# The next batch's layer norm and transposes, moved to other places of an attention kernel's fixed order

## The chip, the cores and the metric

One Trainium2 chip, one core of it. The metric is the device time in microseconds (us) of one execution. The kernel before was timed three times: 2115.77, 2119.26 and 2119.72 us, median 2119.26.

## The reference

Eight batches (graphs) of 1024 tokens with 512 features; 16 heads of 32 features. A token attends to those tokens for which its row of `adj` is 1.

```python
h = relu(layernorm(x))                     # over the 512 features
q, k, v = h @ Wq + bq, h @ Wk + bk, h @ Wv + bv
scores = einsum(q, k) * 32 ** -0.5, -inf where adj == 0
out = softmax(scores) @ v                  # per head
return x + (out @ Wo + bo)
```

## The kernel before

`fast_attention` does the work (a second function, `general_attention`, runs only if a check at the end finds the inputs too large; here its instructions are skipped). Every engine has its own program, written by hand as the same sequence of steps, and the engines meet through semaphores (`wait_ge`, `then_inc`).

**Units and steps.** A batch is four units (`UNITS`, `up` = 0 to 3) of four heads each. A unit is 32 steps (`TILES`, `j` = 0 to 31): two sweeps of 16, one for each half of the queries; within a sweep a step is one tile of 128 keys (`kt`, 0 to 7) for one pair of heads. Batch 0 is written out, batches 1 to 6 are a loop (`Fori`), batch 7 is written out again, so the kernel returns to the start of the loop's body five times.

**The attention of a step.** TensorE (PE) multiplies the scores of step j+1 while it is in step j (`scores`, L679, two matmuls of 512 columns). VectorE (DVE) subtracts the mask and writes the tile to an eight-slot ring (`masked`, L903), ScalarE (ACT) takes the exponential in place (`exp`, L768), GpSimd (POOL) adds four of the eight key tiles up (`sums`, L1077). The products with v (`weighted`, L692, "p0" to "p7") and the row sums (`denominators`, L703, "dA", "dB", "d6", "d7") come as blocks at fixed steps of a sweep; `BLOCKS` puts them at r = 6, 10, 14, 16 and 18, so the last two lie in the next sweep or in the next unit:

```python
BLOCKS = {6: ("p0", "p1"), 10: ("p2", "p3", "dA"), 14: ("p4", "p5"), 16: ("p6", "dB", "d6"), 18: ("p7", "d7")}
```

They are float32 products; each that the code writes stands as two records in the profile.

**The chunks.** Everything else of PE is put in pieces between these steps, after the blocks of a step. Unit u computes, as chunks, what unit u+1 needs: q and k for its four heads (`PROJ`: 12 matmuls of 512 columns for each half of the tokens, so 48 in all, L652), v (96 matmuls of 128 columns, L659) and a bound on the norms (`NORMS`, L662). Units 0 and 1 also multiply the output projection of the batch before ("y", eight chunks of 12, L666). Unit 3 also transposes the next batch's normalised x ("t", eight chunks of four transposes, L648), since its own q, k and v are those of the next batch's unit 0. `chunk_list` gives the order of a unit's chunks, `chunk_plan` the step of every piece: t chunks by the table `T_AT`, the others spread evenly over the steps `SLOTS` (steps 1 to 28 with no block), in unit 3 over `AFTER_T` (those from 13 on). Two PSUM banks serve the chunks by turns, so a chunk waits until the one two before it has been read.

**After a chunk.** `high` on ACT (L774 for t, L780 for q and k, L784 for v) writes the fp16 upper part in the chunk's last step, `low` on DVE the remainder (L912 for t one step later, L916 for q and k two steps later), `square` on ACT (L792) one step after a q or k chunk. q and k then travel: three steps after the second half of q or of k, SyncE (SP) waits for `low` and stores the part to DRAM (`store_parts`, L505); five steps after, it waits for that store and loads it back in another layout by four transfers of 256 KB (`load_stack`, L510). The first scores of the next unit, issued in step 31, wait for all eight of these loads.

**The next batch's x.** `x_in` has four slots for eight tiles of tokens. SP loads tiles (`load_x`, L501), DVE computes statistics (`statistic`, L935) in unit 2, steps 1, 3, ..., 15, and the means in step 21, ACT the reciprocal deviations in step 23, DVE the shifts in step 25. ACT normalises in place (`normalise`, L817) in steps 27 to 30 of unit 2 (tiles 0 to 3) and 5 to 8 of unit 3 (tiles 4 to 7). Each statistic and each transpose is followed, one step later on SP, by a wait for it and the load of another tile into the slot. ACT also turns the next batch's adjacency into the mask (`to_mask`, L823): eight tiles in steps 17 to 30 of unit 3, eight in steps 1 to 13 of unit 0.

Of the kernel before, what the change touches and what calls it, by code (L numbers as in the profile page):

```python
# [4 lines left out]
B, S, D, H, P = 8, 1024, 512, 16, 128  # L5
# [286 lines left out]
NORMS_AT = 29  # L292
T_AT = [1, 3, 4, 5, 7, 8, 9, 11]
AFTER_T = [j for j in SLOTS if j >= 13]
STATS_AT = [2 * t + 1 for t in range(QT)]
MEANS_AT, RSTD_AT, SHIFT_AT = 21, 23, 25
NORMALISE_AT = {(2, 27): 0, (2, 28): 1, (2, 29): 2, (2, 30): 3, (3, 5): 4, (3, 6): 5, (3, 7): 6, (3, 8): 7}
# [4 lines left out]
def chunk_list(up, first, last):  # L302
    if up == UNITS - 1:
        return [] if last else [("t", t) for t in range(QT)] + PROJ + [NORMS]
# [23 lines left out]
def chunk_plan(up, first, last):  # L328

    chunks = [c for c in chunk_list(up, first, last) if c != NORMS]  # L330
    if not chunks:
        return {}
    plan = spread_out([c for c in chunks if c[0] != "t"], AFTER_T if up == UNITS - 1 else SLOTS)
    if up == UNITS - 1:
        plan.update({at: [("t", t, 0, PIECES["t"])] for t, at in enumerate(T_AT)})
    return {**plan, NORMS_AT: [(*NORMS, 0, PIECES["n"])]}

# [49 lines left out]
def fast_attention(nc, x, adjT, Wq, bq, Wk, bk, Wv, bv, Wo, bo, ident, headones, out, parts, flag):  # L387
    ctx = ExitStack()
    with ctx:
# [109 lines left out]
        def _(sp):  # L499
# [49 lines left out]
            def graph(b, first, last):  # L549
                for up in range(UNITS):  # L550
                    U = unit_no(b, up)
                    for j in range(TILES):
# [26 lines left out]
                        if up == 2:  # L579
                            for t, at_ in enumerate(STATS_AT):  # L580
                                if at_ == j - 1:
                                    sp.wait_ge(s["x_stats"], (b + 1) * QT + t + 1)
                                    load_x(b + 1, (t + X_SLOTS) % QT)
                        if up == UNITS - 1:
                            for t, at_ in enumerate(T_AT):
                                if at_ == j - 1:
                                    sp.wait_ge(s["chunk_ready"], chunk_no(ALL, b, up, first, ("t", t)) + 1)
                                    load_x(*((b + 1, t + X_SLOTS) if t + X_SLOTS < QT else (b, t + X_SLOTS - QT)))
# [174 lines left out]
        def _(act):  # L763
# [62 lines left out]
            def graph(b, first, last):  # L826
                for up in range(UNITS):
                    U = unit_no(b, up)
                    for j in range(TILES):
# [20 lines left out]
                        if up == 2 and j == RSTD_AT:  # L850
                            rstds(b + 1)
# [34 lines left out]
        def _(dve):  # L886
# [74 lines left out]
            def graph(b, first, last):  # L961
                for up in range(UNITS):
                    U = unit_no(b, up)
                    for j in range(TILES):
# [16 lines left out]
                        if up == 2 and not last:  # L981
                            if j in STATS_AT:
                                statistic(b, first, b + 1, STATS_AT.index(j))
                            if j == MEANS_AT:
# [155 lines left out]
```

## Time and profile before

| what | us |
|---|---|
| median of three executions | 2119.26 |
| the profiled execution | 2117.94 |
| its span, from the first to the last record | 2116.0 |
| PE busy | 1947.0 (92%) |
| DVE busy | 1545.7 (73%) |
| ACT busy | 1478.1 (70%) |
| POOL busy | 1295.6 (61%) |
| SP's transfers (of 16 engines' span) | 34.7% |
| mean granted clock of TensorE | 0.978 of full speed |

The profiled execution's own time is 1.9 us above its span and 1.3 us below the median. A matmul's end is modelled, so a busy PE is not a PE at its peak; here its matmuls follow one another at the spacing that the chain of waits shows for them, and the time that PE is not busy is where it waits. In the traces `L12` is line 12 of the kernel, `tile<-tiles` what an instruction writes and reads.

### The profile page before, as it was taken

How to read it: one execution, taken by the hardware profiler on the slowest of the kernel's cores; microseconds unless marked ns; L12 is line 12 of the kernel's file. 1: busy time of each engine (PE TensorE's matmuls, PEld its weight loads, DVE VectorE, ACT ScalarE, POOL GpSimd, SP SyncE). 2: the span in 40 equal slices, each digit the busy share in tenths (PEclk: the TensorE clock that was granted, in tenths of full speed). 3: DMA queues.
4: the chain of work that ended last, by engine and by line, in shares of the span. 5: the costliest groups of instructions: out<-in, count | busy, mean ns of one | idle time of the engine just before them, and what ended most of it. 6: DMA issues, size and time to landing. Idle time of an engine off the chain costs nothing.

```text
span 2116.0 us, 40441 instructions
## 1 busy us (share of the span) xinstructions
PE 1947.0 (92%) x14336; PEld 779.1 (37%) x14336; DVE 1545.7 (73%) x1587; ACT 1478.1 (70%) x1765; POOL 1295.6 (61%) x581
## 2 busy tenths in 40 slices
PE   3799999999899998999989999899989999999987
PEld 2333334333344333443334433343333333333422
DVE  5688857787667875778757787578866688677783
ACT  3577866778667786568866788667876678666772
POOL 0367748566567655657656576475656676475674
PEclk9999999999999999999999999999999999999998
DMA  5423234232443324333342334413444233441212
GB/s 175 120 80 94 87 105 135 61 110 76 116 120 89 101 76 126 95 91 95 101 125 75 91 105 116 126 55 91 114 117 111 74 96 97 110 130 46 61 31 80
DMA packets 103222, 206.61 MB, mean 98 GB/s; under 512 B 11616, under 2 KB 11744, under 8 KB 103008
## 3 DMA queue, kind: packets, MB, share of 16 engines
q1 hardware_dynamic: 103008, 203.80, 34.7%
q8 instruction: 129, 2.11, 0.4%
q14 instruction: 85, 0.70, 0.1%
HBM read 153.43 MB, written 50.33 MB: 96 GB/s over the span
## 4 chain that ended last, share of the span: by engine, by line
PE 75%; DVE 7%; DMA 6%; issue 6%; ACT 3%; POOL 1%; SPq 1%; DVEq 0%; ACTq 0%; POOLq 0%
PE ps L692 19%; PE ps L679 19%; PE ps L652 13%; PE ps L703 10%; PE ps L666 6%; PE ps L659 6%; DVE ring L903 4%; DMA k_stack<-k_parts 3%; DMA k_parts<-k_part 2%; ACT ring L768 1%; ACT hT_hi L774 1%; DVE oT_lo L958 1%; DVE k_part L916 1%; POOL acc L1077 1%; SPq L510 1%
## 5 line engine op out<-in xcount | busy, mean ns | idle before, releaser
L903 DVE TENSOR_TENSOR ring<-ps,mask 128x1024 f32<-128x1024 f32 x1024 | 1235.9, 1219 | 492.9 <-PE ps L679 479.7
L768 ACT ACTIVATE ring<-ring 128x1024 f32<-128x1024 f32 x1024 | 1068.3, 1051 | 445.8 <-DVE ring L903 435.5
L1077 POOL TENSOR_TENSOR acc<-ring 128x1024 f32<-128x1024 f32 x256 | 604.4, 2373 | 768.7 <-ACT ring L768 768.5
L679 PE MATMUL ps<-q_stack,k_stack 128*128 128x512 f16 x2048 | 614.5, 385 | 104.8 <-DVE ring L903 47.4
L1077 POOL TENSOR_TENSOR acc<-acc,ring 128x1024 f32<-128x1024 f32 x256 | 611.5, 2410 | 0.0
L692 PE MATMUL ps<-ring,v_sb 128*32 128x512 f32 x4096 | 517.3, 612 | 0.0
L679 PEld LDWEIGHTS ps<-q_stack,k_stack 128*128 128x128 f16 x2048 | 157.3, 98 | 505.4 <-DVE ring L903 240.4
L692 PEld LDWEIGHTS ps<-ring,v_sb 128*32 128x32 f32 x4096 | 101.5, 110 | 257.1 <-issue 229.6
L703 PE MATMUL ps<-acc,ones 128*32 128x512 f32 x1024 | 137.7, 606 | 0.0
L703 PE MATMUL ps<-ring,ones 128*32 128x512 f32 x1024 | 134.6, 595 | 0.0
L659 PE MATMUL ps<-wv_hi,hT_lo 128*128 128x128 f16 x1024 | 105.6, 219 | 0.0
L659 PE MATMUL ps<-wv_lo,hT_hi 128*128 128x128 f16 x1024 | 104.5, 219 | 0.0
L659 PE MATMUL ps<-wv_hi,hT_hi 128*128 128x128 f16 x1024 | 101.7, 219 | 0.0
L823 ACT ACTIVATE mask<-edges,big 128x512 bf16<-128x512 uint32 x120 | 85.3, 711 | 10.9 <-DMA edges<-adjT 10.9
L1085 POOL TENSOR_TENSOR x_in<-x_in,bo_row 128x512 f32<-128x512 f32 x56 | 77.8, 1405 | 21.9 <-DMA x_in<-x 21.9
L796 ACT ACTIVATE rden<-ps 128x512 f32<-128x512 f32 x64 | 38.2, 598 | 69.0 <-PE ps L703 69.0
L652 PE MATMUL ps<-hT_hi,wq_hi 128*128 128x512 f16 x256 | 72.2, 385 | 8.5 <-DVE hT_lo L912 8.4
L666 PE MATMUL ps<-wo_hi,oT_hi 128*128 128x512 f16 x256 | 70.0, 383 | 9.6 <-DVE k_part L916 5.0
L659 PEld LDWEIGHTS ps<-wv_hi,hT_hi 128*128 128x128 f16 x1024 | 71.3, 98 | 18.5
L659 PEld LDWEIGHTS ps<-wv_lo,hT_hi 128*128 128x128 f16 x1024 | 70.8, 98 | 10.9
L652 PE MATMUL ps<-hT_hi,wk_lo 128*128 128x512 f16 x256 | 74.7, 379 | 0.0
L659 PEld LDWEIGHTS ps<-wv_hi,hT_lo 128*128 128x128 f16 x1024 | 70.6, 98 | 10.5
(80 smaller groups left out, 1591.1 us busy)
## 6 DMA issues: line engine op xcount, KB each, us to landing
x_in<-x SPq DMA_DIRECT2D x168, 256.0 KB, 2.7
edges<-adjT SPq DMA_DIRECT2D x128, 256.0 KB, 3.0
q_stack<-q_parts SPq DMA_DIRECT2D x128, 256.0 KB, 4.9
k_stack<-k_parts SPq DMA_DIRECT2D x128, 256.0 KB, 4.9
q_parts<-q_part SPq DMA_DIRECT2D x32, 512.0 KB, 2.9
k_parts<-k_part SPq DMA_DIRECT2D x32, 512.0 KB, 3.2
out<-x_in SPq DMA_DIRECT2D x56, 256.0 KB, 2.1
ring<-x SPq DMA_DIRECT2D x2, 1024.0 KB, 6.7
```

Source lines behind the costliest of these rows:

```text
L652: i = nc.tensor.matmul(bank, w[WQ if kind == "q" else WK][:, c, cols], h[:, c, t * HALF:(t + 1) * HALF], start=m == 0, stop=m == 3 * DC - 1)
L659: i = nc.tensor.matmul(bank[:, tt * P:(tt + 1) * P], h[:, c, tok], w[WV][:, c, cols], start=km == 0, stop=km == 3 * DC - 1)
L666: i = nc.tensor.matmul(bank, o[:, c, t * P:(t + 1) * P], w[WO][:, c, :], start=m == 0, stop=m == 3 * DC - 1)
L679: i = nc.tensor.matmul(ps_s(j)[:, hh, :], stack["k"][:, up % 2, h, kt * P:(kt + 1) * P], stack["q"][:, up % 2, h, half * HALF:(half + 1) * ...
L692: i = nc.tensor.matmul(ps[h * DH:(h + 1) * DH, BANK_O, :], v_sb[:, up % 2, kt, h * DH:(h + 1) * DH], head_of(ring[:, slot_of(kt, h // 2), ...
L703: i = nc.tensor.matmul(ps[h * DH:(h + 1) * DH, BANK_D, :], ones[:], head_of(tile, h), start=term == TERMS[0], stop=term == TERMS[-1], tile ...
L768: nc.scalar.activation(tile, tile, ACT.Exp, scale=SCALE / UP / UP).then_inc(s["prob_ready"], 1)
L796: nc.scalar.activation(rden[:], ps[:, BANK_D, :], ACT.Ln).then_inc(s["ln_done"], 1)
L823: nc.scalar.activation(mask[:, kt, half * HALF:(half + 1) * HALF], edges[:, i % EDGE_SLOTS, :].bitcast(U32), ACT.Relu, bias=big[:], scale= ...
L903: nc.vector.tensor_tensor(ring[:, slot_of(kt, pair), :].rearrange("p (a n) -> p a n", n=HALF), ps_s(j), mask[:, kt:kt + 1, half * HALF:(ha ...
L1077: nc.gpsimd.tensor_tensor(acc[:, group, pair, :], first_of, ring[:, slot_of(kt, pair), :], ALU.add).then_inc(s["sum_done"], 1)
L1085: nc.gpsimd.tensor_tensor(tile, tile, bo_row[:], ALU.add).then_inc(s["x_biased"], 1)
```

## The change

It moves work in the order and alters none of it. Statistics go to unit 1 (steps 13 to 29), the means to its step 31, deviations and shifts to steps 1 and 3 of unit 2. Tiles 0 to 3 are normalised in unit 2 at steps 5, 7, 9, 11, tiles 4 to 7 at steps 23, 25, 27, 29. Six transposes go to unit 2 (steps 19 to 29, every second one) and two stay in unit 3 (steps 1 and 3). In unit 2 the projections are therefore packed into the slots up to step 17, with the norms in step 18; in unit 3 they are spread over the slots from step 5 on. The loads of x follow their statistics and transposes on SP. Units 0 and 1 keep their chunks.

```diff
-NORMS_AT = 29
-T_AT = [1, 3, 4, 5, 7, 8, 9, 11]
-AFTER_T = [j for j in SLOTS if j >= 13]
-STATS_AT = [2 * t + 1 for t in range(QT)]
-MEANS_AT, RSTD_AT, SHIFT_AT = 21, 23, 25
-NORMALISE_AT = {(2, 27): 0, (2, 28): 1, (2, 29): 2, (2, 30): 3, (3, 5): 4, (3, 6): 5, (3, 7): 6, (3, 8): 7}
+STATS_AT = {(1, 13): 0, (1, 17): 1, (1, 20): 2, (1, 23): 3, (1, 24): 4, (1, 25): 5, (1, 27): 6, (1, 29): 7}
+MEANS_AT, RSTD_AT, SHIFT_AT = (1, 31), (2, 1), (2, 3)
+NORMALISE_AT = {(2, 5): 0, (2, 7): 1, (2, 9): 2, (2, 11): 3, (2, 23): 4, (2, 25): 5, (2, 27): 6, (2, 29): 7}
+T_AT = {(2, 19): 0, (2, 21): 1, (2, 23): 2, (2, 25): 3, (2, 27): 4, (2, 29): 5, (3, 1): 6, (3, 3): 7}
+SLOTS_OF = [SLOTS, SLOTS, [j for j in SLOTS if j <= 17], [j for j in SLOTS if j >= 5]]
+NORMS_AT = [29, 29, 18, 29]
...
 def chunk_list(up, first, last):
+    ts = [] if last else [("t", t) for (u, _), t in T_AT.items() if u == up]
     if up == UNITS - 1:
-        return [] if last else [("t", t) for t in range(QT)] + PROJ + [NORMS]
+        return [] if last else ts + PROJ + [NORMS]
+    if up == 2:
+        return PROJ + [NORMS] + ts
...
-                        if up == 2:
-                            for t, at_ in enumerate(STATS_AT):
-                                if at_ == j - 1:
-                                    sp.wait_ge(s["x_stats"], (b + 1) * QT + t + 1)
-                                    load_x(b + 1, (t + X_SLOTS) % QT)
+                        if (up, j - 1) in STATS_AT:
+                            t = STATS_AT[up, j - 1]
+                            sp.wait_ge(s["x_stats"], (b + 1) * QT + t + 1)
+                            load_x(b + 1, (t + X_SLOTS) % QT)
+                        if (up, j - 1) in T_AT:
+                            t = T_AT[up, j - 1]
+                            sp.wait_ge(s["chunk_ready"], chunk_no(ALL, b, up, first, ("t", t)) + 1)
+                            load_x(*((b + 1, t + X_SLOTS) if t + X_SLOTS < QT else (b, t + X_SLOTS - QT)))
```

How rows of the order stand, at three places of the loop's body. `REGISTER_ALU` and `ISA` rows compute the numbers that a wait or an address is made of.

VectorE in steps 24 and 25 of unit 1, where the second half of k gets its lower part (`k_part`), before:

```order
L900 REGISTER_ALU
L902 REGISTER_ALU
L903 TENSOR_TENSOR ring<-ps,mask 128x1024
L901 REGISTER_ALU
L902 REGISTER_ALU
L903 TENSOR_TENSOR ring<-ps,mask 128x1024
L910 REGISTER_ALU
L916 SCALAR_TENSOR_TENSOR k_part<-ps,b_up,k_part 128x512
```

and of the change:

```order
L902 REGISTER_ALU
L904 REGISTER_ALU
L905 TENSOR_TENSOR ring<-ps,mask 128x1024
L493 ISA
L937 BN_STATS stats<-x_in 128x6
L903 REGISTER_ALU
L904 REGISTER_ALU
L905 TENSOR_TENSOR ring<-ps,mask 128x1024
L937 BN_STATS stats<-x_in 128x6
L912 REGISTER_ALU
L918 SCALAR_TENSOR_TENSOR k_part<-ps,b_up,k_part 128x512
```

Two statistics now stand ahead of the lower part of k. One more stands in step 23, ahead of these rows.

ScalarE in steps 27 and 28 of unit 2, before:

```order
L768 ACTIVATE ring<-ring 128x1024
L814 REGISTER_ALU
L490 ISA
L817 ACTIVATE x_in<-x_in,shift,rstd 128x512
L766 REGISTER_ALU
L768 ACTIVATE ring<-ring 128x1024
L839 REGISTER_ALU
L784 ACTIVATE v_sb<-ps 128x512
L817 ACTIVATE x_in<-x_in,shift,rstd 128x512
```

and of the change in steps 23 and 24 of the same unit (`hT_hi` is the upper part of a transposed tile):

```order
L770 ACTIVATE ring<-ring 128x1024
L841 REGISTER_ALU
L776 ACTIVATE hT_hi<-ps 128x4x128
L493 ISA
L819 ACTIVATE x_in<-x_in,shift,rstd 128x512
L768 REGISTER_ALU
L770 ACTIVATE ring<-ring 128x1024
```

An exponential, the upper part of a tile and a normalisation come together in steps 23, 25, 27 and 29, an exponential and an upper part in steps 19 and 21.

SyncE's queue between the second half of k and the next unit's loads, unit 3, before:

```order
L505 DMA k_parts<-k_part 128x2048
L594 REGISTER_ALU
L516 ISA
L516 DMA edges<-adjT 128x512
L510 DMA k_stack<-k_parts 32x4x1024 x4
```

and unit 1 of the change, where the same transfers stand between loads of x:

```order
L504 DMA x_in<-x 128x512
L562 REGISTER_ALU
L508 DMA k_parts<-k_part 128x2048
L584 REGISTER_ALU
L504 DMA x_in<-x 128x512
L513 DMA k_stack<-k_parts 32x4x1024 x4
```

In unit 1 before, the store and the four loads of k stood with nothing between them. In unit 3 the change keeps the rows shown but puts the store in step 23 and the loads in step 25, where they were in steps 27 and 29.

## Rows read from the trace of the kernel before

**Rows 1.** The page: engines' busy us (section 1), the chain (section 4)
```profile
PE 1947.0 (92%) x14336; PEld 779.1 (37%) x14336; DVE 1545.7 (73%) x1587; ACT 1478.1 (70%) x1765; POOL 1295.6 (61%) x581
...
PE 75%; DVE 7%; DMA 6%; issue 6%; ACT 3%; POOL 1%; SPq 1%; DVEq 0%; ACTq 0%; POOLq 0%
```

**Rows 2.** Windows, units 2, 3: length; PE, PEld, DVE, ACT, POOL busy; clock
```profile
1204.17:1258.77 54.60, 53.34 (x420) 20.88 (x416) 47.76 (x58) 42.20 (x51) 38.03 (x16) 1.00 0.37 97
1258.77:1327.31 68.54, 58.58 (x452) 24.11 (x448) 48.45 (x48) 54.98 (x71) 38.10 (x17) 0.98 0.43 116
```

**Rows 3.** Waits over the span: us in total, times, the longest
```profile
PE ps L679 <- DMA k_stack<-k_parts: 42.0, 9, 9.3
```

**Rows 4.** Timeline, unit 3's end, batch 4's start: start, length, what, idle before
```profile
1055.88 0.34 SPq L505 DMA_DIRECT2D k_parts<-k_part  x1
...
1061.96 1.74 SPq L510 DMA_DIRECT2D k_stack<-k_parts  x4
...
1070.05 1.03 PE L679 MATMUL ps<-q_stack,k_stack 128*128 128x512 f16 x2 [4.76 <-DMA k_stack<-k_parts]
...
1073.94 1.03 PE L679 MATMUL ps<-q_stack,k_stack 128*128 128x512 f16 x2 [2.85 <-issue]
```

**Rows 5.** Timeline, end of unit 1 and start of unit 2, batch 4
```profile
1193.23 0.74 DVE L916 SCALAR_TENSOR_TENSOR k_part<-ps,b_up,k_part 128x512 f16<-128x512 f32 x1
...
1194.00 0.34 SPq L505 DMA_DIRECT2D k_parts<-k_part  x1
...
1196.64 2.57 SPq L510 DMA_DIRECT2D k_stack<-k_parts  x4
...
1204.17 1.04 PE L679 MATMUL ps<-q_stack,k_stack 128*128 128x512 f16 x4
...
1206.07 2.19 ACT L768 ACTIVATE ring<-ring 128x1024 f32<-128x1024 f32 x2 [0.91 <-DVE ring L903]
```

**Rows 6.** Windows: step 0 twice, transposes, unit 1 thrice, unit 3 twice
```profile
1073.94:1079.85 5.91, 5.91 (x27) 1.62 (x27) 1.23 (x1) 1.67 (x2) 0.00 (x0) 0.55 0.12 37
1204.40:1207.85 3.45, 3.45 (x28) 0.87 (x27) 2.96 (x3) 2.47 (x3) 0.00 (x0) 1.00 0.00 0
1772.00:1797.00 25.00, 20.85 (x132) 7.03 (x130) 20.29 (x21) 22.84 (x29) 15.12 (x8) 0.93 0.32 96
1143.43:1166.58 23.15, 23.15 (x147) 7.95 (x143) 16.68 (x16) 15.89 (x17) 14.49 (x7) 1.00 0.10 35
1166.58:1175.25 8.67, 8.67 (x52) 3.39 (x49) 6.34 (x6) 5.29 (x6) 4.25 (x2) 1.00 0.27 94
1175.25:1204.17 28.92, 28.92 (x263) 13.23 (x262) 22.02 (x22) 21.00 (x25) 18.74 (x8) 1.00 0.45 110
1258.77:1282.40 23.63, 19.50 (x136) 6.91 (x133) 19.75 (x21) 22.04 (x29) 13.77 (x7) 1.00 0.35 101
1291.00:1319.89 28.89, 28.89 (x255) 13.75 (x254) 19.36 (x20) 23.23 (x32) 18.74 (x8) 1.00 0.45 129
```

**Rows 7.** The chain in order of time: start, us, what
```profile
1004.72 0.44 PE ps L648 x4
...
1032.80 1.51 PE ps L652 x7
...
1052.28 1.23 PE ps L659 x22
```

**Rows 8.** Lines by form, whole span: busy us, mean ns, idle before
```profile
L768 ACT ACTIVATE ring<-ring 128x1024 f32<-128x1024 f32 x1024 | 1068.3, 1051 | 445.8 <-DVE ring L903 435.5
...
L817 ACT ACTIVATE x_in<-x_in,shift,rstd 128x512 f32<-128x512 f32 x56 | 44.9, 803 | 0.0
...
L796 ACT ACTIVATE rden<-ps 128x512 f32<-128x512 f32 x64 | 38.2, 598 | 69.0 <-PE ps L703 69.0
...
L774 ACT ACTIVATE hT_hi<-ps 128x512 f16<-128x512 f32 x64 | 37.4, 584 | 12.1 <-PE ps L648 11.7
...
L935 DVE BATCH_NORM_STATS2 stats<-x_in 128x6 f32<-128x512 f32 x56 | 38.2, 683 | 0.0
```

More of the change, by code:

```diff
@@ L332, in chunk_plan @@
         return {}
[L333 to L336, printed above, removed]
+    plan = spread_out([c for c in chunks if c[0] != "t"], SLOTS_OF[up])
+    plan.update({at: [("t", t, 0, PIECES["t"])] for (u, at), t in T_AT.items() if u == up and ("t", t) in chunks})
+    return {**plan, NORMS_AT[up]: [(*NORMS, 0, PIECES["n"])]}
 def chunk_ends(up, first, last):
@@ L578, in graph @@
                             load_x(b + 1, j)
-                        if up == 2:
-                            for t, at_ in enumerate(STATS_AT):
-                                if at_ == j - 1:
-                                    sp.wait_ge(s["x_stats"], (b + 1) * QT + t + 1)
-                                    load_x(b + 1, (t + X_SLOTS) % QT)
+                        if (up, j - 1) in STATS_AT:
[6 more added lines that the diff above has]
+                            load_x(*((b + 1, t + X_SLOTS) if t + X_SLOTS < QT else (b, t + X_SLOTS - QT)))
                         if up == UNITS - 1:
[L585 to L588, printed above, removed]
                             if j in (6, 8):
@@ L849, in graph @@
                             continue
-                        if up == 2 and j == RSTD_AT:
+                        if (up, j) == RSTD_AT:
                             rstds(b + 1)
@@ L980, in graph @@
                                 .then_inc(s["limits_ready"], 1)
[L981 to L984, printed above, removed]
+                        if not last:
+                            if (up, j) in STATS_AT:
+                                statistic(b, first, b + 1, STATS_AT[up, j])
+                            if (up, j) == MEANS_AT:
                                 means(b + 1)
-                            if j == SHIFT_AT:
+                            if (up, j) == SHIFT_AT:
                                 shifts(b + 1)
@@ L1044, in _ @@
             o_low(U, UNITS - 1)
-            base = chunks_before(ALL, B - 1, UNITS - 1, False)
+            base = chunks_before(ALL, B - 1, UNITS - 1, False) - count("t", chunk_list(2, False, False))
             for t in range(QT):
```

## The prediction

> **What bounds the kernel now.** I read the page first. TensorE (PE) is busy for 92% of the span, and 75% of the chain that ended last is PE's; 6% are transfers [rows 1]. So PE's own work is the bound in most places, and what a reordering can win is the time in which PE is not working, or works slowly. The windows show where that is. Units 2 and 3 hold the same attention work, and their chunks differ by the eight transposes alone, yet unit 2 takes 54.60 us and unit 3 68.54 [rows 2]. The list of waits names one cause: the first scores of a unit wait for k from DRAM, 42.0 us in nine places, the longest 9.3 (taken as the program's first, before which nothing can run) [rows 3]. The other 32.7 us are some 4.7 at each of the seven ends of a unit 3. The timeline shows one: k is stored at 1055.88, its loads are issued from 1061.96, six us later, and PE starts at 1070.05; then the second pair of scores starts only at 1073.94, with PE idle for 2.85 and nothing that the profile could name ("issue") [rows 4]. That second gap lies at the return of the loop. At the end of unit 1 the store takes 2.64 us (1194.00 to 1196.64), the loads are issued by 1198.9 (1196.64 + 2.57 less one issue of 0.34), and PE goes on at 1204.17 [rows 5]. In unit 3 the last load was issued at 1063.4 and needed 6.7; here it needed 5.3 at most. So at the end of unit 1 k arrives just in time, and I count no slack there.
>
> A third loss is the clock. After the 4.76 us without work, step 0's blocks took 5.91 us at a granted clock of 0.55; the same blocks at 1.00 took 3.45 [rows 6]. The fourth is the transposes' stretch. Its price needs the prices of PE's work: a projection matmul 1.51 / 7 = 0.216 us, a matmul of v 1.23 / 22 = 0.056, the four transposes of a tile 0.44 [rows 7]. Unit 1 is PE-bound (busy through all three of its windows), so its windows less its chunks are a unit's bare steps: up to the scores of step 12, 23.15 - 39 x 0.216 = 14.7; from there to those of step 17, 8.67 - 22 x 0.216 = 3.9; the rest 28.92 - 23 x 0.216 - 96 x 0.056 = 18.6, with the norms [rows 6]. Unit 3's first part needs 14.7 + 7 x 0.44 = 17.8 us of PE and took 23.63, in which ScalarE (ACT) was busy for 22.04: ACT set the pace, with exponentials, normalisations and upper parts side by side.
>
> **The change, part by part.** I sum units 2 and 3 together, by the same three parts.
> Unit 2: 14.7 + 44 x 0.216 = 24.2; 3.9 + 4 x 0.216 + 74 x 0.056 = 8.9; 18.6 + 22 x 0.056 + 6 x 0.44 = 22.4 (the norms only change their place). Sum 55.5.
> Unit 3: 14.7 + 18 x 0.216 + 2 x 0.44 = 19.5; 3.9 + 17 x 0.216 = 7.6; 18.6 + 13 x 0.216 + 96 x 0.056 = 26.8. Sum 53.9.
> Together 109.4 for PE alone, against 123.1 now. k's wait is gone in that: its second half is stored in step 23, and from there the transfers need 2.6 for the store where nothing else is in the queue (6.1 where it is), 1.4 for the issues and 6.7 for the landing, 10.7 to 14.2. Steps 23 to 31 are nine of the fifteen that hold 26.8, about 16. What is late next is the loop's return, which stays.
>
> But ACT bounds the new stretch as it bounds the old one. From step 17 of unit 2 to the first projection of unit 3 (step 5, which needs the last tile's lower part) ACT has 19 exponentials at 1.05, 4 normalisations at 0.80, 8 upper parts at 0.58, one of v at about the same, and two reciprocals of two instructions at 0.60 [rows 8]: 20.0 + 3.2 + 4.7 + 0.6 + 2.4 = 30.9. I add 1.0 for gaps (now ACT idles 1.6 of 23.63 in such a stretch), 1.9 by which it trails PE at the start (scores at 1204.17, exponential at 1206.07 [rows 5]) and 0.9 for the last lower part: 34.7. PE needs 22.4 + half of 14.7 + 0.43 + 0.88 = 31.1. So 3.6 us are lost. In unit 3's last part ACT has the same work as now (23.23 in 28.89 [rows 6]) while PE gets 4.5 us less to do; the two are then about level, and I charge 0.7. Units 2 and 3: 109.4 + 3.6 + 0.7 = 113.7, a gain of 9.4 in each of seven batches, 65.8. Bounds: 13.7 if ACT's work hides in PE's lead, 5.4 if the transposes cost what they cost now (below).
>
> Unit 0: with no wait before it, step 0's blocks should run at full clock, 2.5 us saved; PE still idles for the 2.85 of the loop's return, so I take 2.0 (bounds 0 and 2.5). Against it ACT now pays its own return in the open, and unit 0 begins with ACT behind: 0.8 (0 to 3). Net 1.2 x 7 = 8.4.
>
> Unit 1: DVE gets eight statistics of 0.68 and is busy for 22 of 28.9 us in the last part, so the work itself hides. Its place does not: two of them now stand ahead of k's lower part. Less the 0.4 that DVE idles there, the store starts 1.0 later, and its traffic meets loads of x, 0.3. With no slack this is a wait of 1.3 us before unit 2's first scores (bounds 0 and 4), in six batches 7.8. In batch 0, whose unit 1 has no output products to cover the statistics, I take 2. The means in step 31 lie in that wait. What leaves unit 2's front (statistics) and unit 3 (loads of x ahead of mask loads) costs nothing and gives nothing: PE sets the pace there.
>
> Sum: -65.8 - 8.4 + 7.8 + 2.0 = -64.4, from the profiled execution's 2117.94 to 2053.5. The median lies 1.3 above that execution: **2055 us**.
>
> **A rule against it.** The stretch of seven transposes from 1772 to 1797 shows a clock of 0.93, a part of it at 1.2 instead of 2.4 GHz, while the like stretch from 1258.77 shows 1.00 [rows 6]. The Trainium skill ("TensorE: Matmul & The Clock Gate", Part 4: PE-mode transpose) says that transposes do not count as PE being busy for the clock. The traces agree in part: it falls in some of these stretches, and not in others. And the skill ("Runtime: NRT & Kernel Launch", Instruction fetch mechanics) says that a taken branch out of the prefetched window stalls its engine for a fetch: by this every engine, not PE alone, would pay at the loop's return, as I charged ACT.
>
> **The rivals.**
> 1. *ACT's load hides and k keeps its slack.* PE alone: 13.7 x 7 + 2.0 x 7 = 110 less, with half of unit 1's charge 2013 to 2040, say 2020. For it: PE may lead ACT by several steps before a block needs the exponential. Against: it did not help in the old stretch. 0.14.
> 2. *The transposes stay a serial chain* (PE, ACT, DVE, bank free). They cost 23.63 - 17.8 = 5.8 for seven now, 0.83 each, so 6.6 for eight, and 1.5 for the projection behind them, in place of my 3.6 + 0.7: 4 more in seven batches, 2083. Against: they are two steps apart instead of one. 0.20.
> 3. *k's wait moves to the end of unit 1.* Three loads of x stand around its store. If the store takes 3.4 longer as in unit 3 [rows 4, 5], the loads 3 longer, with 1.0 of delay and a fall of the clock at 2.5, each of six batches loses 9.9 in place of 1.3: 2107. It would eat the whole gain only from 12 us per batch. 0.08.
> 4. *Slower: the clock stays at its lower level through unit 2's sparse tail.* PE has no projections from step 18 on; if all 22.4 us of work there run at half speed, they take 22.4 more, some 3 hidden by ACT: 19.4 x 7 on top, 2190. It decides from 9.2 us lost per batch, half of that stretch and more. Against: 0.93 and 1.00 in stretches with more transposes and as few other matmuls. This is what the skill's rule on transposes would do if it held strictly. 0.06.
>
> **How the numbers follow.** My forecast, 2040 to 2072, has 0.52; the rivals 0.14, 0.20, 0.08 and 0.06. The range 2025 to 2095 takes in the forecast, most of rival 2 and the upper half of rival 1. About 0.2% (4 us) is what a measurement here tells from no change. Faster 0.92, within it 0.02 (the end of rival 3), slower 0.06.
>
> **What would show it.** Right: no wait for k before unit 0's scores and a clock near 1.00 in step 0's blocks; the 2.9 us at the loop's return still there; units 2 and 3 at 57 to 60 and 54 to 57 us with ACT over 90% busy from step 17 of unit 2; a wait for k of 1 to 2 us before unit 2. Wrong: that wait at 4 or more, or units 2 and 3 together under 111 or over 118.

## The result, and the profile after

Median of four executions 2086.02 us (2085.39 to 2087.57), against 2118.67 (2115.77 to 2119.72) for the kernel before in the same job: ratio 0.9849, 95% interval 0.9837 to 0.9862. It is faster, by 32.7 us, which is half of the forecast 64. The time lies inside the stated range of 2025 to 2095 and outside the forecast of 2040 to 2072. The profiled execution took 2085.51 us. The page, as [rows 1]:

```profile
PE 1932.5 (93%) x14336; PEld 776.5 (37%) x14336; DVE 1557.3 (75%) x1587; ACT 1478.1 (71%) x1765; POOL 1302.1 (62%) x581
...
PE 76%; DVE 7%; issue 6%; DMA 5%; ACT 2%; POOL 1%; SPq 1%; DVEq 0%; ACTq 0%; POOLq 0%
```

The shares of the page hardly moved; the change is in the units. These are windows of batch 4, in the columns of [rows 2] and [rows 6]: unit 2, unit 3, unit 2's last part (scores 17 to the end), unit 3's first part (scores 0 to 12) and its last.

```profile
1181.76:1243.31 61.55, 56.81 (x440) 23.44 (x441) 47.63 (x48) 48.33 (x63) 38.52 (x16) 1.00 0.29 79
1243.31:1299.70 56.39, 54.36 (x428) 21.75 (x424) 45.46 (x43) 45.52 (x56) 37.85 (x16) 1.00 0.38 104
1215.07:1243.31 28.24, 23.50 (x192) 9.13 (x190) 21.51 (x24) 21.73 (x28) 18.74 (x8) 1.00 0.32 83
1243.31:1265.35 22.04, 20.01 (x134) 6.60 (x130) 18.64 (x18) 18.08 (x21) 14.29 (x6) 1.00 0.16 48
1272.94:1299.70 26.76, 26.76 (x253) 12.25 (x251) 20.91 (x20) 22.13 (x29) 18.11 (x8) 1.00 0.61 160
```

Unit 3 fell from 68.54 to 56.39, unit 2 rose from 54.60 to 61.55 [rows 2]. In unit 2's last part PE is idle for 4.7 of 28.24 us while no other engine is full: DVE and ACT are each busy for under 22 (ACT for 77% of it, where the prediction looked for over 90%). The lines of PE in that window name what it waits for (the row's last column):

```profile
L681 PE MATMUL ps<-q_stack,k_stack 128*128 128x512 f16 x30 | 9.0, 382 | 4.7 <-DVE ring L905 4.7
...
L650 PE MATMUL ps<-idt,x_in 128*128 128x128 f32 x24 | 3.6, 273 | 0.0
```

All of it stands before scores, released by DVE's mask subtraction, and none before the transposes. The waits for k over the whole span, as [rows 3] (42.0 us in nine places there). What is left is the program's first scores and the starts of six units 2; none stands before a unit 0:

```profile
PE ps L681 <- DMA k_stack<-k_parts: 13.6, 7, 9.5
```

The timeline of unit 3's end and the loop's return, as [rows 4]:

```profile
1286.51 0.36 SPq L508 DMA_DIRECT2D k_parts<-k_part  x1
...
1290.20 2.17 SPq L513 DMA_DIRECT2D k_stack<-k_parts  x4
...
1299.71 0.61 PE L681 MATMUL ps<-q_stack,k_stack 128*128 128x512 f16 x2
...
1302.08 0.60 PE L681 MATMUL ps<-q_stack,k_stack 128*128 128x512 f16 x2 [1.76 <-issue]
...
1303.49 1.02 PE L705 MATMUL ps<-acc,ones 128*32 128x512 f32 x3
...
1305.21 0.12 PEld L705 LDWEIGHTS ps<-acc,ones 128*32 128x32 f32 x3 [1.61 <-issue]
```

The loads of k go out 9.5 us ahead and PE starts unit 0 without waiting for them. What stays are two gaps at the return for which the profile names no cause ("issue"); the second is 1.61 us between weight loads and 0.70 between PE's matmuls. The window of step 0's blocks, which has one matmul of the scores less than that of [rows 6] (from the same matmul on it is 4.98 us, against 5.91 at clock 0.55 before):

```profile
1302.31:1307.06 4.75, 4.05 (x26) 0.78 (x25) 1.99 (x2) 2.98 (x4) 0.00 (x0) 1.00 0.22 64
```

The end of unit 1, as [rows 5]:

```profile
1170.34 0.73 DVE L918 SCALAR_TENSOR_TENSOR k_part<-ps,b_up,k_part 128x512 f16<-128x512 f32 x1
...
1171.10 0.33 SPq L508 DMA_DIRECT2D k_parts<-k_part  x1
...
1173.98 2.76 SPq L513 DMA_DIRECT2D k_stack<-k_parts  x4
...
1181.77 1.03 PE L681 MATMUL ps<-q_stack,k_stack 128*128 128x512 f16 x4 [0.55 <-DMA k_stack<-k_parts]
```

The sum by units, each from its first scores to those of the next unit, over the two profiled executions (what is not listed, the program's start and end and two units, comes to 0.3 us):

| part | forecast, us | measured, us |
|---|---|---|
| units 2 and 3, batches 0 to 6 | -65.8 | -38.1 |
| unit 0, batches 1 to 7 | -8.4 | -10.4 |
| unit 1 | +9.8 | +9.4 |
| unit 2 of batch 7 | 0 | +6.4 |
| sum | -64.4 | -32.7 |

### The profile page after: what moved, and what is told of

It is laid out like the page before. It is cut to its first block, busy times and chain, and to the rows that moved or that the text cites. A ratio compares the mean times of both kernels' runs of the same rounds, so it can differ in the third digit from the quotient of the medians.

```text
span 2083.6 us, 40441 instructions
## 1 busy us (share of the span) xinstructions
PE 1932.5 (93%) x14336; PEld 776.5 (37%) x14336; DVE 1557.3 (75%) x1587; ACT 1478.1 (71%) x1765; POOL 1302.1 (62%) x581
## 4 chain that ended last, share of the span: by engine, by line
PE 76%; DVE 7%; issue 6%; DMA 5%; ACT 2%; POOL 1%; SPq 1%; DVEq 0%; ACTq 0%; POOLq 0%
PE ps L694 20%; PE ps L681 19%; PE ps L654 15%; PE ps L705 10%; PE ps L668 7%; PE ps L661 6%; DVE ring L905 4%; DMA k_stack<-k_parts 2%; DMA k_parts<-k_part 1%; SPq L513 1%; DMA edges<-adjT 1%; ACT hT_hi L776 1%; DVE k_part L918 1%; POOL acc L1079 1%; ACT ring L770 1%
## 5 line engine op out<-in xcount | busy, mean ns | idle before, releaser
L681 PE MATMUL ps<-q_stack,k_stack 128*128 128x512 f16 x2048 | 610.4, 382 | 85.2 <-DVE ring L905 61.4
L694 PE MATMUL ps<-ring,v_sb 128*32 128x512 f32 x4096 | 509.1, 604 | 0.0
L661 PE MATMUL ps<-wv_hi,hT_lo 128*128 128x128 f16 x1024 | 100.8, 219 | 0.0
L654 PE MATMUL ps<-hT_hi,wq_hi 128*128 128x512 f16 x256 | 72.7, 388 | 14.2 <-DVE hT_lo L914 14.2
L661 PEld LDWEIGHTS ps<-wv_lo,hT_hi 128*128 128x128 f16 x1024 | 71.0, 98 | 14.2
L654 PE MATMUL ps<-hT_hi,wk_hi 128*128 128x512 f16 x256 | 72.5, 379 | 2.1 <-DVE q_part L918 2.1
L654 PE MATMUL ps<-hT_lo,wq_hi 128*128 128x512 f16 x256 | 74.1, 383 | 0.0
```

What stands on the lines that cost most here:

```text
L654: i = nc.tensor.matmul(bank, w[WQ if kind == "q" else WK][:, c, cols], h[:, c, t * HALF:(t + 1) * HALF], start=m == 0, stop=m == 3 * DC - 1)
L661: i = nc.tensor.matmul(bank[:, tt * P:(tt + 1) * P], h[:, c, tok], w[WV][:, c, cols], start=km == 0, stop=km == 3 * DC - 1)
L681: i = nc.tensor.matmul(ps_s(j)[:, hh, :], stack["k"][:, up % 2, h, kt * P:(kt + 1) * P], stack["q"][:, up % 2, h, half * HALF:(half + 1) * ...
L694: i = nc.tensor.matmul(ps[h * DH:(h + 1) * DH, BANK_O, :], v_sb[:, up % 2, kt, h * DH:(h + 1) * DH], head_of(ring[:, slot_of(kt, h // 2), ...
```

## The experiments

Twelve kernels were run. "A part" is a stretch between two scores, as in the windows. Where one time stands, the kernel was executed once; where an interval stands, it was timed several times beside the kernel before. The mean of batches 1 to 6 stands for a unit where nothing else is said.

**x1_pack: only unit 2's projections are packed.**

```diff
-    plan = spread_out([...], AFTER_T if up == UNITS - 1 else SLOTS)
+    plan = spread_out([...], AFTER_T if up == UNITS - 1 else [j for j in SLOTS if j <= 17] if up == 2 else SLOTS)
-    return {**plan, NORMS_AT: [...]}
+    return {**plan, 18 if up == 2 else NORMS_AT: [...]}
```

> The kernel before with one part of the change: unit 2's projections packed into the slots up to step 17 and its norms in step 18; statistics, normalisations and transposes stay where they were. Theory A (an emptied stretch is not free: steps without chunk work run at VectorE's pace of about 1.2 us, because only two score buffers exist, whatever ScalarE has to do besides): unit 2 goes from 54.6 to about 59 us, as unit 2 of the last batch does in the changed kernel (54.0 to 60.5 with no transposes in it), so about 35 us slower, near 2153. Theory B (the loss in unit 2's tail comes from the normalisations and upper parts that were put there): without them the tail costs what PE's matmuls cost, 19.8 in place of 25.6, unit 2 gets 53 us, and the time is 2105 to 2120.

Measured 2163.17 (2162.13 to 2164.68), ratio 1.0214 (1.0197 to 1.0231). Unit 2 takes 60.5 us in place of 54.6, unit 3 is as before. So the packing alone, with no transpose in unit 2, costs 5.9 us. Its last part in batch 4 and in batch 7, and PE's scores in that of batch 4:

```profile
1259.92:1287.10 27.18, 22.34 (x168) 6.48 (x165) 19.16 (x28) 18.90 (x23) 18.00 (x8) 0.94 0.21 47
2046.20:2072.04 25.84, 20.73 (x170) 6.33 (x167) 18.66 (x18) 17.62 (x19) 18.20 (x8) 1.00 0.19 42
```
```profile
L679 PE MATMUL ps<-q_stack,k_stack 128*128 128x512 f16 x30 | 8.6, 384 | 4.8 <-DVE ring L903 4.8
```

The idle time is spread over the steps without chunks, 0.5 to 1.1 us at a place, and is as large in batch 7 (5.1). What makes the part 1.3 us longer in batch 4 is the clock: it read 0.94, and one block of products ran slowly. The block in batch 4 and the same in batch 7:

```profile
1271.93 3.49 PE L692 MATMUL ps<-ring,v_sb 128*32 128x512 f32 x16
...
2058.23 1.92 PE L692 MATMUL ps<-ring,v_sb 128*32 128x512 f32 x16
```

The changed kernel's clock read 1.00 in this part in six of the seven batches with transposes. Without the slow block unit 2 takes 59.15 us, as one batch of x5_act below shows, so some 4.5 of the 6.9 us that the changed kernel's unit 2 lost are the packing. Its six transposes added 2.8 us of PE's work to the part and filled none of the idle time (4.8 us without them, 4.7 with them).

**x5_act, x6_dve, x6b_both: which engine sets that pace.** On x1_pack, in steps 17 to 31 of unit 2 alone, ScalarE's exponential takes 512 of its 1024 columns (x5), or DVE's mask operation does (x6), or both (x6b). The kernels leave out half of the probabilities there (x5, x6b) or half of the masked scores (x6, x6b), and the mask operation is a comparison in place of the subtraction. Where both are halved, the logarithm of the row sums also gets a small bias.

```diff
+                tile = ring[:, slot_of(*divmod(r, PAIRS)), 0:HALF if up == 2 and j >= 17 else 2 * HALF]   # x5, x6b
+                n = 1 if up == 2 and j >= 17 else 2                                                     # x6, x6b
+                nc.vector.tensor_tensor(ring[..., 0:n * HALF]..., ps_s(j)[:, 0:n], ...to_broadcast([P, n, HALF]), ALU.is_lt ...)
```

> x1_pack with ScalarE's exp halved in steps 17 to 31 of unit 2 (it takes 512 of the 1024 columns; the mask operation there is a comparison of the same size, so the other columns and with them the output mean nothing). x1_pack: 2163 us, and unit 2's last part (steps 17 to 31) 27.2 us with PE busy for 22.4. Theory A, the part runs at the pace of the hand-over between PE and DVE (two score buffers, one mask subtraction of 1.2 us a tile): ScalarE is not in that ring, the part stays at 26.5 to 27.2 us and the kernel at 2157 to 2164. Theory B, it runs at ScalarE's pace (1.06 us a tile beside its other operations, 21 us busy in the part): the part falls to 24 to 25 us and the kernel to about 2163 - 8 x 2.5 = 2143.

> x1_pack with DVE's mask operation halved in steps 17 to 31 of unit 2 (a comparison of 512 of the 1024 columns, the rest keeps stale values, so the output means nothing). Theory A (pace of the hand-over PE to DVE and back): the steps without chunk work shorten from 1.2 to about 1.06 us or less, where ScalarE's exp is next; the part falls from 27.2 to 24 us (the stall behind the means of step 21 also shrinks), the kernel to about 2163 - 8 x 3 = 2139. Theory B (ScalarE's pace): the part stays above 26.5 and the kernel above 2157.

> x1_pack with both halved in steps 17 to 31 of unit 2 (output means nothing). Theory A and B alike: PE becomes the bound, the part comes to PE's own 22.4 us or a few tenths above (22.4 to 23.2), the kernel to 2163 - 8 x 4.4 = 2128. If it stays above 24, a third thing (POOL's sums, the waits inside the blocks) sets the pace of the emptied steps.

Measured 2162.94, 2144.36 and 2136.32 us. The last part of unit 2 in batch 4, in the order x5, x6, x6b:

```profile
1257.99:1285.41 27.42, 22.45 (x168) 6.42 (x165) 21.07 (x28) 14.03 (x24) 18.72 (x8) 0.94 0.21 47
```
```profile
1249.69:1272.04 22.35, 20.70 (x169) 6.31 (x166) 13.45 (x28) 16.91 (x21) 14.94 (x7) 1.00 0.28 58
```
```profile
1245.39:1267.73 22.34, 20.68 (x168) 6.30 (x165) 13.09 (x28) 13.59 (x24) 15.28 (x7) 1.00 0.26 59
```

Halving ACT's work changes next to nothing (27.18 became 27.42 in this batch). The mean fell from 27.20 to 26.93 because the slow block was absent in two of the batches; at clock 1.00 the part is 25.84 us with ACT's work whole (batch 7 above) and with it halved:

```profile
1521.42:1547.26 25.84, 20.88 (x168) 6.16 (x166) 21.07 (x28) 14.04 (x24) 18.73 (x8) 1.00 0.22 50
```

Halving DVE's takes 4.8 us off, and ACT's on top of it nothing more. Of the 4.8 us, 3.2 are PE's idle time before scores (4.8 fell to 1.65) and 1.6 the slow block, which did not come in either kernel. Theory A holds: there are two score buffers, scores(j+1) wait for the subtraction of tile j-1, and this takes 1.22 us. Steps with 0.6 us of scores and nothing else cannot follow each other faster than DVE's subtractions do (1.13 us apart in x1_pack). With chunks in each step the same DVE work is hidden.

The kernels gained 19 and 27 us, where I expected 24 and 35: in x6 the eight units 2 gave 35 us and the seven units 3 took 13 back, in x6b 40 and 11. The trace of x6 names what took it back. In unit 3's first part of batch 4 PE waits before a block of row sums for GpSimd, which it does nowhere there in x1_pack:

```profile
PE ps L703 <- POOL acc L1078: 1.8, 1, 1.8
```

Over seven batches this is 12.3 us; in x6b it is 1.4 us a batch. So the next engine behind DVE is GpSimd, at the turn to unit 3.

**x9_adve and x10_aboth: the same cuts in the changed kernel** (x9: DVE's, x10: both; steps 17 to 31 of unit 2; the kernels leave out what x6 and x6b do).

> The changed kernel with DVE's mask operation halved in steps 17 to 31 of unit 2 (a comparison of 512 of the 1024 columns, the rest keeps stale values, so the output means nothing). Changed kernel: 2086 us, unit 2's last part (steps 17 to 31) 28.4 us with PE busy for 23.7 and ScalarE for 24.3. Theory A, the hand-over at DVE's pace is what the forecast missed: as in the variant with packed projections alone, the part falls to within 1 us of PE's own work, 24 to 25 us, unit 2 to about 57.5, and the kernel to 2086 - 8 x 4 = 2054, which is the forecast. Theory B, ScalarE is full there (24.3 us, with transposes and normalisations that the other variant had not): the part stays above 26.5 and the kernel above 2070.

> The changed kernel with both DVE's mask operation and ScalarE's exp halved in steps 17 to 31 of unit 2 (output means nothing). With DVE's alone halved the part went from 28.4 to 26.0 us and PE was still idle for 2.9 of it, against 0.2 of PE's work left uncovered in the variant without transposes there. Theory A (two limits in a row: first the hand-over with DVE, then ScalarE, which has 24.3 us of work in that part in the changed kernel): with both halved the part comes to 23.2 to 24.5 us and the kernel to 2071 - 7.5 x 2 = 2056. Theory B (the rest is a chain of the transposes themselves, PE waiting for normalise, high part and low part of the tile two before): the part stays above 25.3 and the kernel above 2065.

Measured 2070.89 and 2054.92 us. The last part went from 28.24 to:

```profile
1209.51:1235.55 26.04, 23.08 (x192) 9.18 (x189) 14.06 (x24) 21.33 (x28) 17.65 (x8) 1.00 0.36 90
```
```profile
1197.15:1222.50 25.35, 23.08 (x192) 9.21 (x189) 14.66 (x24) 16.84 (x28) 18.06 (x8) 1.00 0.35 91
```

x9 is a miss for both of its theories. In the changed kernel DVE's pace is worth 2.2 us of the part, ACT's 0.7 on top. PE still idles for 2.3, in three places, each before the scores behind a second transpose. So a part of the loss belongs to the transposes' own chain, as theory B of x10 says. The rows of DVE name a link of it, in x9 and in x10:

```profile
L915 DVE SCALAR_TENSOR_TENSOR hT_lo<-ps,hT_hi 128x512 f16<-128x512 f32 x6 | 4.2, 692 | 5.0 <-ACT hT_hi L776 5.0
```
```profile
L915 DVE SCALAR_TENSOR_TENSOR hT_lo<-ps,hT_hi 128x512 f16<-128x512 f32 x6 | 4.2, 692 | 2.7 <-ACT hT_hi L776 2.7
```

DVE stands before a tile's lower part until ACT has written the upper part, and the next subtraction, for which PE waits, stands behind it in DVE's order. In the changed kernel DVE waits there for 1.9 us. That this wait and not another link is what costs was not tried by a run of its own. x10's total is no evidence for A: of its 16 us against x9 only about 7.5 lie in unit 2 and about 6 in unit 1, which the edit does not touch (k came earlier there), and the kernel before ran at 2112.15 on x10's chip and at 2119.88 on x9's.

**x2_kearly: the kernel before with unit 3's q and k packed into steps 13 to 21 and v behind them, nothing else moved.**

```diff
+        plan = {**spread_out(PROJ[:4], [13, 15, 17, 19, 20, 21]), **spread_out(PROJ[4:], [23, 24, 25, 27, 28])}
```

> The kernel before with q and k of unit 3 packed into steps 13 to 21 and v behind them in steps 23 to 28; nothing moves to another unit. Theory A (all that the change gained is the wait for k at the end of unit 3 and what follows it): the 4.7 us wait goes seven times (33), the cold blocks of step 0 in batches 1 and 7 (4) and 1.3 us of the loop's return five times (6.5): about 2075, 11 us faster than the whole change, with unit 3 near 64 us. Theory B (unit 3 gains because its work is spread thinner, not because k comes early): the packed q and k cost what the wait gives back, 2100 to 2119.

Measured 2087.69 (2082.24 to 2089.48), ratio 0.9853 (0.9831 to 0.9874). Unit 3 goes from 68.75 to 64.6, units 1 and 2 stay. One line in the plan brings as much as the whole change (0.9849): what that change won beyond k's wait it paid back in unit 2. The transfers of k in x2_kearly:

```profile
1035.87 0.74 DVE L917 SCALAR_TENSOR_TENSOR k_part<-ps,b_up,k_part 128x512 f16<-128x512 f32 x1
...
1037.75 0.36 SPq L517 DMA_DIRECT2D edges<-adjT  x1
1038.22 0.36 SPq L506 DMA_DIRECT2D k_parts<-k_part  x1
...
1043.56 2.37 SPq L511 DMA_DIRECT2D k_stack<-k_parts  x4
...
1051.39 0.60 PE L680 MATMUL ps<-q_stack,k_stack 128*128 128x512 f16 x2 [0.85 <-DMA k_stack<-k_parts]
```

0.85 us of the wait are left: the store stands on SP behind an edge load that waits for a mask operation.

**x12_order: the same, with SP's order in unit 3 changed.**

```diff
-                        for kind, t in ending_at(up, first, last, j - 3, "qk"):
+                        for kind, t in ending_at(up, first, last, j - (2 if up == UNITS - 1 else 3), "qk"):
...
-                        for kind, t in ending_at(up, first, last, j - 5, "qk"):
+                        for kind, t in ending_at(up, first, last, j - (4 if up == UNITS - 1 else 5), "qk"):
```

> x2_kearly (2087.7 us) with SP's order changed in unit 3 alone: the stores of q and k one step earlier and the stack loads one step earlier against the edge loads, which wait for ScalarE's mask operations. In x2_kearly k's low part is done at 1036.65, its store goes out at 1038.22, behind an edge load that waited for a mask operation, the loads at 1043.56, and the last lands 0.1 us before the scores that wait for it. Theory A (k's store and loads stand behind SP's waits): the loads go out 1.5 to 2.5 us earlier, the last step of unit 3 goes from 3.27 to 2.4 us, unit 3 from 64.6 to 63.7 and the kernel to 2088 - 7 x 0.9 = 2081.5. Theory B (the transfers share the same DMA engines and come out at the same rate whatever their order): unit 3 and the kernel stay within 2 us of x2_kearly.

Measured 2075.27 (2073.11 to 2077.49), ratio 0.9824 (0.9804 to 0.9845), the lowest of the kernels that compute the whole result. In x12_order:

```profile
1281.86 0.74 DVE L917 SCALAR_TENSOR_TENSOR k_part<-ps,b_up,k_part 128x512 f16<-128x512 f32 x1
1282.63 0.34 SPq L506 DMA_DIRECT2D k_parts<-k_part  x1
...
1286.63 2.27 SPq L511 DMA_DIRECT2D k_stack<-k_parts  x4
...
1296.46 0.61 PE L680 MATMUL ps<-q_stack,k_stack 128*128 128x512 f16 x2
```

The store follows the lower part at once (0.03 us after its end; 1.61 in x2_kearly), the loads go out 9.8 us ahead of the scores in place of 7.8, and no wait is left. Unit 3 is at 63.7, as theory A had it. A second gain came with it: scores(0) to scores(2) at the returns fell from 9.6 us in x2_kearly to 8.0. The interval overlaps those of x2_kearly and of the changed kernel, and the kernel before ran at 2112.15 on that chip, 5.6 us below its 2117.76 on x2_kearly's; so of the 12.4 us between the two medians about half may be the chip. In the profiles, first scores to last, x12_order takes 1960.3 us, the changed kernel 1973.2.

**x3_stats: the changed kernel with the last five statistics of unit 1 in steps 22, 26, 27, 28, 30**, none between k's last matmul and its lower part.

```diff
-STATS_AT = {(1, 13): 0, (1, 17): 1, (1, 20): 2, (1, 23): 3, (1, 24): 4, (1, 25): 5, (1, 27): 6, (1, 29): 7}
+STATS_AT = {(1, 13): 0, (1, 17): 1, (1, 20): 2, (1, 22): 3, (1, 26): 4, (1, 27): 5, (1, 28): 6, (1, 30): 7}
```

> The changed kernel with the statistics of tiles 3 to 7 in steps 22, 26, 27, 28 and 30 of unit 1 (in place of 23, 24, 25, 27, 29), so that none stands ahead of k's lower part in steps 24 and 25. Theory A (two statistics ahead of the lower part delay k's store, with no slack behind it): unit 1 returns from 62.2 to 60.8 us, 1.4 x 6 = 8 us faster than the change, 2078. Theory B (VectorE's total in unit 1, or the loads of x beside the store, is what costs): unit 1 stays at 62, 2084 to 2088.

Measured 2083.77 (2079.5 to 2087.09), ratio 0.9834 (0.9815 to 0.9852). Unit 1 goes from 62.2 to 61.4 (60.8 before the change): a stall of 0.54 us of PE behind DVE's lower part of k is gone. k still lands 0.1 us before the scores, and in batch 4 its loads take 7.9 us from the first issue to the last landing, against 7.4 before the change; so the rows put the other half of unit 1's price to the traffic beside k's loads, which no run took away. The gain in the median, 2.3 us, is inside the intervals.

**x4_bal: the changed kernel with less packing**: projections up to step 21 of unit 2, four transposes there and four in unit 3.

```diff
-NORMALISE_AT = {..., (2, 23): 4, (2, 25): 5, (2, 27): 6, (2, 29): 7}
-T_AT = {(2, 19): 0, (2, 21): 1, (2, 23): 2, (2, 25): 3, (2, 27): 4, (2, 29): 5, (3, 1): 6, (3, 3): 7}
-SLOTS_OF = [SLOTS, SLOTS, [j for j in SLOTS if j <= 17], [j for j in SLOTS if j >= 5]]
-NORMS_AT = [29, 29, 18, 29]
+NORMALISE_AT = {..., (2, 28): 4, (2, 29): 5, (2, 30): 6, (2, 31): 7}
+T_AT = {(2, 24): 0, (2, 25): 1, (2, 27): 2, (2, 28): 3, (3, 0): 4, (3, 1): 5, (3, 3): 6, (3, 4): 7}
+SLOTS_OF = [SLOTS, SLOTS, [j for j in SLOTS if j <= 21], [j for j in SLOTS if j >= 7]]
+NORMS_AT = [29, 29, 23, 29]
```

> The changed kernel with PE's chunk work more evenly over units 2 and 3: projections of unit 2 up to step 21, norms in 23, four transposes in steps 24 to 28, four in steps 0 to 4 of unit 3, projections of unit 3 from step 7, normalisations 4 to 7 in steps 28 to 31. Theory A (each step without 0.7 us of chunk work wastes that much of PE): units 2 and 3 together fall from 117.9 to about 114.5, 3.4 x 7 = 24 us faster than the change, near 2062. Theory B (the serial chain of transposes costs 0.8 us each wherever they stand): no gain, 2082 to 2090, or slower because they now stand one step apart.

Measured 2106.44 (2104.16 to 2108.71), ratio 0.9951 (0.9934 to 0.9968): a miss. Unit 2 won 2.5 us (59.0), and unit 3 lost 5 (61.4 in place of 56.4): its first part took 24.3 in place of 22.05, with PE standing for 2.06 us before the scores of step 7, behind DVE, after transposes one step apart; and with q and k later the wait for k came back (1.8 us).

**x7_mix and x8_q0: the kernel before with unit 3's work interleaved**, q's (and in x7 k's) first half between the transposes, since it needs only tiles 0 to 3. x8 also moves three normalisations.

```diff
-T_AT = [1, 3, 4, 5, 7, 8, 9, 11]
+T_AT = [1, 3, 4, 5, 9, 12, 13, 15]      # x7: order T0-3, q0, T4, k0, T5-7, q1, k1, v
+T_AT = [1, 3, 4, 5, 7, 11, 12, 13]      # x8: order T0-4, q0, T5-7, q1, k, v
+MIXED = [(7, ("q", 0, 0, 6)), (8, ("q", 0, 6, 12)), (9, ("k", 0, 0, 5)), (11, ("k", 0, 5, 12)), ...]      # x7
+MIXED = [(8, ("q", 0, 0, 6)), (9, ("q", 0, 6, 12)), (15, ("q", 1, 0, 8)), (17, ("q", 1, 8, 12), ("k", 0, 0, 4)), ...]      # x8
```

> The kernel before with unit 3's chunks interleaved: the first halves of q and k, which need only transposes 0 to 3, in steps 7 to 11, transposes 4 to 7 at steps 9, 12, 13, 15, the second halves in steps 17 to 21, v in 23 to 28; unit 2 and its statistics stay. Theory A (steps without chunk work are dead time at DVE's pace, so work spread evenly over the slots is what counts): unit 3 64.6 (x2_kearly) -> 57 to 59 us, since its front no longer stands at DVE's pace and its tail no longer carries 16 us of projections in eleven slots; unit 2 stays 54.6; the kernel 2088 - 7 x 6.5 = 2042, range 2035 to 2055. Theory B (unit 3's length is set by ScalarE, which has the masks, normalisations and both halves' high parts there): unit 3 stays above 62 and the kernel above 2070.

> The kernel before with unit 3 in this order: transposes 0 to 4, q's first half in steps 8 and 9, transposes 5 to 7 at steps 11 to 13, q's second half in 15 and 17, k in 17 to 21, v in 23 to 28; unit 2 and its statistics stay. x7_mix failed by two things that are mended here: k's first half asked for the PSUM bank that q's had two slots before (1.9 to 2.4 us waits), and q's and k's second halves ended within a step of each other, so that their eight stack loads queued behind one another and k's landed 5 us late. Theory A (dead time of steps without chunk work): against x2_kearly (unit 3 64.6) 2.6 us of projections move from the dense part into steps at DVE's pace, so unit 3 comes to 61.5 to 63 and the kernel to 2088 - 7 x 2.5 = 2070, range 2063 to 2078. Theory B (ScalarE is the bound of unit 3's first part, 24 us busy in 24.6): the first part grows by what the last part loses, unit 3 stays at 64 to 65 and the kernel at 2084 or above.

Measured 2122.19 (2116.75 to 2127.58), ratio 1.0015 (1.0001 to 1.0028), and 2109.20 (2108.61 to 2112.07), ratio 0.9956 (0.9939 to 0.9973). Both miss. Unit 3 took 68.7 and 67.6 us. One row of x7, k's first half, which takes the PSUM bank of q's:

```profile
1283.53 1.04 PE L662 MATMUL ps<-hT_hi,wk_hi 128*128 128x512 f16 x4 [1.88 <-DVE q_part L926]
```

Its q and k also ended within a step of each other, their eight loads queued, and the scores waited 4.99 us for k. One row of x8, q's first half, one step behind a transpose:

```profile
1273.20 1.03 PE L661 MATMUL ps<-hT_hi,wq_hi 128*128 128x512 f16 x4 [2.56 <-DVE hT_lo L921]
```

Both put a projection right behind the chunk whose result or bank it needs, and PE, which takes its work in order, stood. x8's scores also waited 1.4 to 2.7 us for k. The two runs tell nothing against theory A, and nothing for it either. Whether unit 3's first part can be filled at all stays open.

## Why the prediction was right or wrong

**The time fell inside the range in part by luck.** The mechanism of the forecast, k's wait gone and ACT as the bound of the new stretch, came in its first half only. The range reached up to 2095 to take in most of rival 2, and 2086 lies there, with a mechanism that is rival 2's in part.

**Right, as put:** k's wait at the end of unit 3 is gone. Packed and spread parts cost what PE's prices say: unit 2's first two parts 24.24 and 9.07 (24.2 and 8.9 forecast), unit 3's middle and last 7.59 and 26.76 (7.6 and 26.8). The 0.7 charged for ACT in unit 3's last part was not needed. Unit 1 lost 1.37 in each of six batches (1.3 forecast), 0.8 of it by DVE's statistics (x3_stats); batch 0's lost 1.0 where I took 2. Unit 0 gained 10.4 in sum (8.4 forecast).

**The step that failed: "PE needs 22.4 ... So 3.6 us are lost".** Unit 2's last part took 28.37 us, unit 3's first 22.05, together 50.4. I had 22.4 + 19.5 + 3.6 = 45.5. The 4.9, less the 0.7 not needed, are 4.2 of the 4.4 us per batch that are missing in units 2 and 3 (118.07 in the mean of batches 1 to 6 against 113.7; over 118 was a sign of being wrong). In the windows of batch 4, 6.8 us of the two parts are PE's idle time, where I charged 3.6, and PE's records fill 43.5, where I had priced 41.9: a pair of scores behind a stop shows 0.60 us, and 0.43 where matmuls follow one another. I compared two totals over the stretch, PE's work and ACT's, and took the larger. But the bound is a hand-over in each step: scores(j+1) wait for DVE on tile j-1. With two buffers PE can't lead, and what a heavy step leaves unused does not help a light one. The experiments size it: in x1_pack 3.2 us of idle time (4.8 us with the slow block) fall away with DVE's operation halved; in the changed kernel 2.2 with DVE's, 0.7 with ACT's, and 2.3 us of PE's idle time before scores stay, behind the transposes' chain. ACT, the bound of the forecast, was busy for 77% of the one part and 82% of the other. In unit 3's first part 1.1 us more are the first projection, which waits for the last tile's lower part (14.2 us in eight places over the span, 6.3 of them at the program's start). "A unit's bare steps" at 18.6 was taken from unit 1, where nearly every step holds a chunk or a block. So it is a price of PE's work, not the length of bare steps.

**The trace of before had the evidence.** Unit 3 of batch 7 has no chunks at all. Its window in the kernel before, up to its last scores, and PE's line in it:

```profile
2024.57:2072.95 48.38, 38.18 (x242) 9.30 (x238) 38.60 (x34) 34.37 (x36) 35.26 (x16) 0.96 0.00 1
```
```profile
L679 PE MATMUL ps<-q_stack,k_stack 128*128 128x512 f16 x62 | 17.3, 388 | 9.7 <-DVE ring L903 9.7
```

It is 48.4 us where my prices give 14.7 + 3.9 + 18.6 = 37.2 for a whole unit: PE idles for 9.7, all before scores and all ended by DVE. I priced bare steps without looking at the one bare unit.

**A term left out: batch 7.** Its unit 2 has no transposes to make room for, but `SLOTS_OF` packs its projections all the same: 54.0 to 60.5 us, +6.4, a fifth of the whole gain. The diff shows it; I counted seven batches.

**Right in size, cause partly wrong: unit 0.** I gave the 2.0 to the clock. Where no loop return lies between, the clock did it: in batches 1 and 7 step 0's blocks went from 6.15 and 4.62 us to 3.45. At the five returns they take 4.9 to 6.1 us, against 4.8 to 5.9 before, so nothing is won there: at three of the returns the clock reads 1.00, and PE stands for 0.6 to 1.0 us inside the blocks; at two it reads 0.68 and 0.72. The interval from scores(0) to scores(1) shrank instead, from 3.6 to 4.1 us to 2.4 to 3.1. The 0.8 that I charged for ACT's own return was sized by no run.

**The rule against the change** ("TensorE: Matmul & The Clock Gate", Part 4, in the Trainium skill). By it the clock should have fallen in unit 2's last part, with six transposes and few other matmuls. It read 1.00 there in six of the seven batches that have them, and 0.94 in one (29.0 us in place of 28.2). In x1_pack, with no transposes in that part, it read 0.94 in seven of eight batches, and in x5_act, whose PE does the same work with the same stops up to the slow block, in four of eight. In x6_dve and x6b_both, where PE is idle for under 2 us, it read 1.00 in all. So here the falls need no transposes; what decides between 0.94 and 1.00 is open. Rival 4 did not come: the clock was low there for some 3 us in one batch.

**The rivals.** Rival 2 gave 2083 and came nearest. Its size was right and its mechanism in part: packing without a transpose costs 4.5 of unit 2's 6.9 us at full clock (5.9 with the slow block). Rival 3 did not come: the wait before unit 2 is 0.55 us in the row above. My lower bound for the gain in units 2 and 3, 5.4 per batch, is what was measured (38.1 / 7). It was the price of rival 2's chain, so this too is in part luck.

## What to carry to other kernels

Before work is packed into one part of a pipelined loop, price the part that it leaves by a stretch of the trace that is already empty, not by the busy engine's work. Where two buffers go back and forth, a step costs at least what the slower engine of the hand-over needs for one buffer (here 1.22 us of DVE's beside 0.6 of PE's), and other work of the faster engine is free up to the difference, some 0.6 us per step, only if it is spread. And if one wait is the target, try first the one line that removes this wait alone: here issuing k earlier gave as much as the whole rearrangement (ratios 0.9853 and 0.9849), and with its store ahead of other waits in the queue perhaps more (0.9824, with an interval that overlaps).

## What was unexpected of the hardware

At the loop's return PE stands between scores(0) and scores(1), for 2.6 to 3.4 us before the change and 1.8 to 2.5 after it, with nothing to wait for that the profile could name. At four of the changed kernel's five returns it stands again within the next blocks, for 0.3 to 1.0 us (0.70 in the rows above, 1.61 between its weight loads). The Trainium skill ("Runtime: NRT & Kernel Launch", Instruction fetch mechanics) says that a taken branch out of the prefetched window stalls for a fetch; a second gap some 2.4 us of work after the first is what the rows add, and what it stands for they don't show. Before the change, with the clock at 0.55 to 0.68 in these blocks, there is no second gap, and they took as long.

The whole return got shorter only when PE no longer waited for k just before it: scores(0) to scores(2) at the five returns takes 9.2 us in the kernel before, behind a wait of 4.6 to 5.0, and 9.6 in x2_kearly, where 0.9 of the wait is left; it takes 8.0 in x12_order and 7.9 in the changed kernel, where none is left. Why a wait of under 1 us costs 1.6 more behind it was not tried.
